# Second state-space layer: each exponents' product of the quad after next placed between quarters of a quad's short products

## The reference, cut to what matters

```
dA = jnp.exp(dt * A)                 # per token and head
def step(state, inp):                # over the tokens
    dA_t, dtx_t, B_t, C_t = inp
    state = state * dA_t[..., None, None] + jnp.einsum('bgcp,bgn->bgcpn', dtx_t, B_t)
    y_t = jnp.einsum('bgn,bgcpn->bgcp', C_t, state)
    return (state, y_t)
```

## Time and profile before

| | us |
|---|---|
| median of 3 runs | 1076.72 |
| lowest, highest run | 1075.82, 1077.52 |
| the profiled execution | 1076.35 |
| its span, first to last instruction | 1075.0 |
| TensorE busy | 1027.3 (96%) |
| VectorE busy | 794.6 (74%) |
| GpSimd busy | 699.0 (65%) |
| ScalarE busy | 615.5 (57%) |
| mean granted TensorE clock | 0.993 |

### The profile page before, as it was taken

The page is one execution under the profiler, slowest core; times in us unless marked ns, Lnnn a source line. Parts: engine busy times, 40 slices in busy tenths (PEclk is TensorE's granted clock), DMA queues, the critical chain, the costliest instruction groups (busy, mean ns, idle before and its releaser), DMA issues.

```text
span 1075.0 us, 23860 instructions
## 1 busy us (share of the span) xinstructions
PE 1027.3 (96%) x9886; PEld 852.1 (79%) x9886; DVE 794.6 (74%) x1191; ACT 615.5 (57%) x954; POOL 699.0 (65%) x685
## 2 busy tenths in 40 slices
PE   7899999999999999999999999999899889999998
PEld 6688888888888888888887888888664577788887
DVE  4689888898888888788876785556849864786454
ACT  5888787776867778777645232223883543432221
POOL 4886786886868868688683488654377223295553
PEclk9899999999999999999999999999999999999999
DMA  3312111121121211111020463302031120253411
GB/s 112 112 71 79 50 60 70 41 80 51 60 69 40 80 52 66 63 40 51 2 70 4 117 231 103 122 32 82 36 91 26 30 71 2 78 175 108 118 55 40
DMA packets 47388, 76.28 MB, mean 71 GB/s; under 512 B 11366, under 2 KB 34258, under 8 KB 47282
## 3 DMA queue, kind: packets, MB, share of 16 engines
q1 hardware_dynamic: 47282, 74.77, 21.9%
HBM read 68.46 MB, written 2.36 MB: 66 GB/s over the span
## 4 chain that ended last, share of the span: by engine, by line
PE 63%; DVE 20%; POOL 8%; ACT 4%; issue 3%; SPq 1%; DMA 1%; DVEq 0%; POOLq 0%; ACTq 0%
PE psum L722 33%; PE psum L960 7%; DVE arena L1742 7%; PE psum L694 4%; PE psum L810 4%; PE psum L802 3%; PE psum L855 3%; DVE arena L1779 2%; PE psum L1074 2%; PE psum L1038 1%; SPq L520 1%; PE psum L1108 1%; DVE v L2048 1%; DVE arena L1798 1%; DVE arena L1806 1%
## 5 line engine op out<-in xcount | busy, mean ns | idle before, releaser
L722 PE MATMUL psum<-vT,split 128*128 128x512 f32 x2136 | 538.5, 402 | 8.1 <-DVE arena L1742 5.5
L722 PEld LDWEIGHTS psum<-vT,split 128*128 128x128 f32 x2136 | 390.8, 189 | 97.1 <-DVE arena L1742 7.0
L1742 DVE SCALAR_TENSOR_TENSOR arena<-psum,arena 128x1023 f32<-128x1023 f32 (+2 forms) x208 | 265.7, 1277 | 76.1 <-ACT arena L1267 52.8
L2200 POOL TENSOR_TENSOR split<-arena,split 128x256 fp32r<-128x256 f32 x178 | 134.7, 770 | 63.5 <-ACT split L1192 63.3
L1267 ACT ACTIVATE arena<-psum,arena 128x512 f32<-128x512 f32 x160 | 109.1, 690 | 73.8 <-PE psum L722 72.9
L2407 POOL TENSOR_TENSOR arena<-arena,bcast 128x512 f32<-128x512 f32 x64 | 85.1, 1332 | 93.1 <-ACT arena L1439 82.0
L1439 ACT ACTIVATE arena<-psum,arena 128x512 f32<-128x512 f32 x72 | 49.5, 687 | 164.1 <-PE psum L722 163.1
L1894 DVE SCALAR_TENSOR_TENSOR arena<-psum,arena 128x512 f32<-128x512 f32 x72 | 53.9, 748 | 101.1 <-POOL arena L2407 100.7
L960 PEld LDWEIGHTS psum<-split_down,split_hid 128*128 128x128 f32 x864 | 112.6, 191 | 9.5 <-DVE split_hid L1907 3.7
L960 PE MATMUL psum<-split_down,split_hid 128*128 128x256 f32 x864 | 115.2, 283 | 3.0 <-DVE split_hid L1907 3.0
L2227 POOL TENSOR_TENSOR arena<-arena,v 128x1021 f32<-128x1021 f32 x32 | 76.5, 2390 | 44.6 <-DVE arena L1742 44.4
(11 more groups left out here) (228 smaller groups left out, 1514.8 us busy)
## 6 DMA issues: line engine op xcount, KB each, us to landing
bcast<-scratch_a SPq DMA_DIRECT2D x32, 512.0 KB, 3.7
bcast<-scratch_e SPq DMA_DIRECT2D x32, 512.0 KB, 4.2
arena<-in_w_a SPq DMA_DIRECT2D x16, 768.0 KB, 4.4
arena<-in_wg SPq DMA_DIRECT2D x36, 128.0 KB, 3.6
arena<-in_wu SPq DMA_DIRECT2D x36, 128.0 KB, 3.5
arena<-in_wd SPq DMA_DIRECT2D x36, 128.0 KB, 4.0
arena<-in_wout_a SPq DMA_DIRECT2D x8, 256.0 KB, 2.6
arena<-in_w_b SPq DMA_DIRECT2D x10, 128.0 KB, 4.7
```

Of the source, the lines that this page charges most:

```text
L722: m = pe.matmul(bank, split[:, t % SPLITS, i, q, :], vT[:, j, q, half * BANK:(half + 1) * BANK], start=(n == 0), stop=(n == 3 * KD - 1))
L1742: dve.scalar_tensor_tensor(out=tile[:, s:T], in0=bank[:, 0:T - s], scalar=cw_a[:, j, i, TAPS - 1 - s:TAPS - s], in1=tile[:, s:T], op0=ALU. ...
L2200: pool.tensor_tensor(split[:, t % SPLITS, 1], raw, split[:, t % SPLITS, 0].bitcast(F32), ALU.subtract).then_inc(sem["split"], 1)
```

## The change

For k = 8 to 13 the four exponents' products of quad k + 2 no longer stand together ahead of quad k's short products. The quad's eight chunks are split into four quarters of two chunks (16 short products, 32 records), and exponents' product j is issued just ahead of quarter j. For k = 10 `finish(1)` therefore comes ahead of all four of them. For k = 14 and 15 there are no exponents left, and the order stays as it was. Quads 0 to 7 are untouched. The number of products, their shapes, the semaphores and the other engines' programs stay the same; the waits of `inside` are issued ahead of its first quarter, behind the first exponents' product.

```
-                def exponents(k):
+                def exponents(k, heads=range(4)):
...
-                    for j in range(4):
+                    for j in heads:
                         bank = open_bank(("D", 4 * k + j))
...
-                def inside(k):
+                def inside(k, chunks=range(NC)):
...
-                    for c in range(NC):
+                    for c in chunks:
                         for j in range(4):
                             for r in range(2):
...
-                    m.then_inc(sem["heads"], 1)
+                    if chunks[-1] == NC - 1:
+                        m.then_inc(sem["heads"], 1)
...
                 for k in range(QUADS):
                     if k == NC - 1:
                         give(k)
-                    for q in quads_ahead(k):
-                        if q < QUADS:
+                    if k < NC:
+                        for q in quads_ahead(k):
                             exponents(q)
                     if k < NC - 1:
                         add_states(k + 1)
                         give(k)
                     if k == NC + 2:
                         finish(1)
-                    inside(k)
+                    if k < NC:
+                        inside(k)
+                    else:
+
+                        for j in range(4):
+                            if k + 2 < QUADS:
+                                exponents(k + 2, (j,))
+                            inside(k, range(2 * j, 2 * j + 2))
```

## The result

The changed kernel took 1089.14 us (median of 22 runs, 1077.1 to 1094.0), the kernel before in the same session 1077.87 us (22 runs, 1074.69 to 1080.3). The ratio is 1.0074, interval 1.0053 to 1.0095: slower by 0.7%, outside the forecast range. The median hides what matters. The runs fall into two groups with nothing between 1079.6 and 1088.0: seven runs at 1077.1 to 1079.5 us with a mean granted clock of 0.990 to 0.993, and fifteen at 1088.0 to 1094.0 us with 0.973 to 0.982. The profiled execution is one of the long group, 1092.15 us with a span of 1090.8.

A forecast was written before the change was run, and what follows sets the result against it. TensorE, busy 96%, was taken as the bound, with quads 9 to 11 held by instruction supply. Added work nets zero up to 870.98, then -0.44 + 0.79 = +0.35 us (+1.34 if the clock drops): 1077.1 us, range 1075.4 to 1079.8.

The forecast's parts named there:

- Quads 12 and 13: Last two interleaved quads, no stops there: quad 13 +0.79 us; quad 12 -0.44 with clock up, +0.55 if it drops.
- Quad 8: First interleaved quad: three exponents' products now follow the wait for the wide tile, so quad 9 starts 1.50 us late.
- The price at the low clock: Quad 12 if the clock drops: 0.60 us exponents' product, 0.42 quarter, 0.15 change back; about 4.3 us in all.
- The extra work went into the stops: Quads 9 to 11: of 4.1 us added, 3.87 go into stops for instruction packets; `finish(2)` unchanged at 870.98, net zero.
- "issue" stops: Three TensorE idle times before 859.34, 866.79 and 870.73, together 3.87 us, read as waits for the next instruction packet.
- The new wait for masks: Quad 11: VectorE masks it until 867.57, so its short products, otherwise due at 867.40, wait some 0.2 us.
- The last stop that was forecast: Quad 11: reaches its packet's end at about 870.4 and waits until 870.73; the 1.17 us stop shrinks to some 0.3.
- the sum: Whole kernel: 0 to 870.98, then +0.35 us with the clock up or +1.34 with the drop; median 1077.1 us.
- The stops do not shrink: Rival, quads 8 to 13: stops are paid per packet wherever it falls, so 5.4 us come on top, 1082.1 us; chance 0.11.
- Packets are asked for later: Rival: waits behind single products make three packets each 2.1 us late, +6 to +7 us, 1083; chance 0.04.

The follow-up runs named there:

- by halves: Changed kernel, but quads 8 to 13 alternate two exponents' products with half the short products: 1076.82 us against 1077.5 before; timed again, 1075.82 against 1077.64.

## Why the prediction was wrong

**The step that failed** is in "Quads 12 and 13": "I take it that the clock stays at 2.4 GHz", and its alternative, a drop priced at 3.4 us in quad 12 alone. The forecast treated the clock as something that quad 12 might lose or keep, and did not ask what the interleaved order itself does to it. The step "Quad 8" had the trigger in hand, "only one is issued ahead of that wait, and three stand behind it", and priced it as time only. The idle time grew from 0.47 to 1.16 us, about two thirds of the runs fell into the long group (15 of 22, 8 of 12), and in both of its profiles the clock fell in quad 8 and stayed down for 34 to 38 us, to the end of quad 12. In place of +0.35 or +1.34 us the profiled run took 14.6 us more in quads 8 to 13. None of the rivals was this. The price at the low clock was also too small: 0.60 + 0.42 + 0.15 = 1.17 us for a lone exponents' product, a quarter and the change back, where 1.34 was measured. It was taken from the rates of quad 12 before, whose exponents' products stand in a row at 0.47 us each (872.91 to 874.79); a lone one takes 0.72 us to the next short product.

**What held.** The kind of price was right: 0.83 us from one exponents' product to the next at the high clock was forecast, 0.82 measured. The extra work went into the stops: none of the "issue" stops is left when all quads are interleaved, 1.25 and 1.98 us of 3.87 in the two profiles by halves, and 2.4 us of extra work in quads 9 to 11 did not move `finish(2)` back (0.5 us earlier). With the idle stretch filled, quad 8's first short product to quad 11's first exponents' product took 11.51 us (857.03 to 868.54), where the forecast has 11.47 (855.50 to 866.97). The new wait for masks was forecast at 0.2 us and is 0.23. The last stop that was forecast, some 0.3 us in quad 11, did not show there, nor with only quads 9 to 11 interleaved. Of the short group of the changed kernel, seven runs, the median is 1078.02 us against 1077.87 for the kernel before: +0.15 us where +0.35 was forecast. So the sum was right for one run in three, as a total: no run of that group was profiled, and +0.15 us is small beside the spread of the runs.

**The rivals.** "The stops do not shrink", 1082.1 us, is refuted by the rows of the kernel with the filled stretch and of the one with only quads 9 to 11 interleaved. That rival leant on the Trainium skill (Runtime: NRT & Kernel Launch, Instruction fetch mechanics), which has the cost of crossing into a new block of instructions mostly hidden; here it was 3.87 us in three stops, and hidden only once TensorE was slowed. "Packets are asked for later" was not seen: by the start of `finish(2)` the last of these packets came 0.5 us earlier with quads 9 to 11 interleaved, and 0.8 us earlier or no earlier by halves.

**What stood ahead of the clock's falls and returns.** In five profiles it falls in quad 8, within the idle stretch (this kernel) or 0.1 to 1.7 us behind its end; in one, with the same stretch, it does not fall. Five quads of interleaved work stood in the low clock without ending it, and so did four exponents' products with `finish(1)` behind them. It came back with four exponents' products followed at once by 128 short records (1.1 us into the short ones in two profiles), and in the four other profiles with a long low clock, this kernel's two among them, in or just behind the first piece of the projection. The Trainium skill (TensorE: Matmul & The Clock Gate, Part 1: The HAM clock gate) says that the gate goes by how busy TensorE has been of late. The traces agree in so far as the falls come with or soon after idle time; but TensorE is listed busy without a gap from 858.5 to 863.8, and its clock is 1.2 GHz all the while. Which property of the interleaved work keeps the clock low was not separated here: its small products and its many changes of kind are candidates, and neither was tested by itself.

## What to carry to other kernels

A stall of TensorE can cost more than its own time if small products interleaved with large ones follow it: put products into an unavoidable wait, or a stretch of products of one kind soon behind it. Do not judge a reordering on TensorE by one profile, since the same program gave 1077 and 1092 us; look at the granted clock of every run. And one profile of a changed rhythm of instructions is not enough either: by halves, two profiles of one program differ by 0.8 us in the same stretch. When stops for instructions bound a stretch, extra work there can be free.

## What was not expected of the hardware

- One program has two well separated times, 1078 and 1090 us. In both profiles of the long one the clock falls in or just behind one idle stretch of 1.2 us, and it stays low for 34 to 38 us.
- Twenty more records of work on TensorE (2.3 us) made the kernel 11.3 us faster in the median (1089.74 to 1078.48).
- Slower work in a stretch bound by packets of instructions can be free or even come out ahead. By halves a quad takes 2.90 us and not 2.53 (872.18 to 875.08), yet `finish(2)` came 16.3 us after quad 8's first exponents' product in one profile and 17.15 in the other, where the kernel before has 17.1. Why the packets came sooner in one of them stays open.
